# Two 64-key attentions of a pair as one walk over 64 tile slots, on one core

## The reference

```python
# second layer: softmax scale 1/sqrt(128); masks are given
sa  = attention(x, x, x, tgt_mask)                  # 16 heads of 8 features, 64 keys
out = layernorm(x + sa)
ca  = attention(ctx, ctx, out, src_mask)            # keys and values from ctx_1024
out = layernorm(out + ca)
# ... feed forward, gated fusion ...
# last layer: softmax scale 1/sqrt(8); no masks
q   = ln(x);  x = x + mha(q, q)
qc  = ln(x);  kv = ln(ctx);  x = x + mha(qc, kv)
# ... top-2 of 8 experts ...
```

## Time and profile before

| | |
|---|---|
| median of 3 runs | 2118.17 us (2116.89 to 2119.68) |
| the profiled execution's own time | 2117.3 us |
| its span in the trace | 2115.7 us |
| granted TensorE clock, mean over the span | 0.896 |
| PE busy in the span | 79% |
| DVE / ACT / POOL busy | 65% / 54% / 46% |

### The profile page before, as it was taken

One profiled execution on the slowest core, in us unless ns is written; L12 is line 12 of the kernel. 1 busy time (PEld: TensorE's weight loads), 2 busy tenths in 40 slices (PEclk: granted clock), 3 DMA queues, 4 the chain that ended last, 5 costly groups with the idle time before them and its releaser, 6 DMA issues. The chain is left out here.

```text
span 2115.7 us, 56320 instructions
## 1 busy us (share of the span) xinstructions
PE 1674.4 (79%) x17626; PEld 1301.0 (61%) x17626; DVE 1370.0 (65%) x4296; ACT 1142.8 (54%) x3291; POOL 963.3 (46%) x1443
## 2 busy tenths in 40 slices
PE   5899999999997799979897854599788972218882
PEld 5788888888866566656665712366566651217771
DVE  2677777777766488857776468677667852226773
ACT  1577777777753365546664322377567740007771
POOL 2344444444424355546665424344334434435773
PEclk9999999999998899989998967799879975559996
DMA  6776666666640222200000000000000000016665
GB/s 184 141 159 146 152 145 150 145 150 145 150 107 0 85 96 96 100 16 16 16 16 4 0 1 0 1 0 0 5 9 11 12 3 31 26 52 199 211 215 156
DMA packets 214507, 166.84 MB, mean 79 GB/s; under 512 B 27344, under 2 KB 188496, under 8 KB 214160
## 3 DMA queue, kind: packets, MB, share of 16 engines
q1 hardware_dynamic: 205840, 142.85, 27.0%
q0 software_dynamic: 8576, 22.88, 3.2%
HBM read 91.92 MB, written 73.76 MB: 78 GB/s over the span
## 5 line engine op out<-in xcount | busy, mean ns | idle before, releaser
L815 POOL TENSOR_TENSOR sb_work<-sb_work,sb_cols 128x512 f32<-128x512 f32 x128 | 134.4, 1050 | 316.2 <-ACT sb_work L1022 201.9
L678 ACT ACTIVATE sb_probs<-sb_probs,sb_work 128x128 f32<-128x128 f32 x512 | 198.7, 407 | 116.3 <-DVE sb_work L603 116.3
L953 DVE TENSOR_REDUCE sb_work<-PS 128x8 f32<-128x512 f32 x256 | 175.3, 685 | 87.2 <-PE PS L858 85.9
L257 POOL TENSOR_SCALAR sb_next_var_eps<-sb_next_moments 128x1 f32<-128x1 f32 (+1 forms) x184 | 43.9, 238 | 339.5 <-DVE sb_next_moments L252 338.8
L836 PE MATMUL PS<-sb_ident,sb_work 128*128 128x128 f32 x1024 | 168.4, 289 | 33.1 <-ACT sb_work L989 28.0
L989 ACT ACTIVATE sb_work<-sb_work 128x512 f32<-128x512 f32 x256 | 161.3, 630 | 60.3 <-DVE sb_work L955 59.2
L955 DVE TENSOR_TENSOR sb_work<-PS,sb_work 128x512 f32<-128x512 f32 x256 | 176.9, 691 | 8.8
L836 PEld LDWEIGHTS PS<-sb_ident,sb_work 128*128 128x128 f32 x1024 | 116.4, 145 | 69.7 <-ACT sb_work L989 55.1
L879 PE MATMUL PS<-sb_v_ones,sb_work 128*64 128x18 f32 x4096 | 146.5, 215 | 3.8 <-ACT sb_work L995 3.7
L879 PEld LDWEIGHTS PS<-sb_v_ones,sb_work 128*64 128x64 f32 x4096 | 134.0, 141 | 22.4 <-issue 10.2
L995 ACT ACTIVATE sb_work<-PS 128x512 f32<-128x512 f32 x256 | 139.8, 595 | 6.1 <-PE PS L836 2.5
(11 more groups left out here) (274 smaller groups left out, 4484.8 us busy)
## 6 DMA issues: line engine op xcount, KB each, us to landing
rel_scratch<-sb_work SPq DMA_DIRECT2D x64, 516.0 KB, 7.9
sb_work<-rel_scratch SPq DMA_DIRECT2D x64, 512.0 KB, 6.6
expert_rows<-sb_blank SPq DMA_DIRECT2D x36, 520.0 KB, 2.9
sb_w_up<-expert_halves SPq DMA_DIRECT2D x23, 512.0 KB
sb_w_down<-expert_halves SPq DMA_DIRECT2D x23, 512.0 KB
expert_halves<-sb_e_halves POOLq DMA_DIRECT2D x16, 512.0 KB, 5.9
sb_work<-expert_rows SPq DMA_DIRECT2D x23, 260.0 KB
sb_e_raw<-e_W POOLq DMA_DIRECT2D x16, 256.0 KB, 6.8
```

The source lines that it names most:

```text
L678: ins = e.activation(probs[:, j], probs[:, j], ACT.Exp, bias=neg_max[:, j:j + 1], scale=-1.0, accum_out=row_sum[:, j:j + 1])
L815: e.tensor_tensor(k_masked[:, u], k_sb[:, u].rearrange("p (b k) -> p b k", b=2).unsqueeze(2) .to_broadcast([P, 2, 4, S]), col("place").uns ...
L953: e.tensor_reduce(top, mine, AX.X, ALU.max).then_inc(sem("att_max_ready"), 1)
```

## The change

`PHASES` has eight entries instead of ten: `(AT, ATT[0:2])` and `(AT, ATT[2:4])` hold a pair each. `walk_pair` takes the place of `walk_late`: it counts n from -2 to 64, and each of the four roles gets the attention that its own tile slot belongs to (slots 0 to 31 the first, 32 to 63 the second). Steps 2 to 29 and 34 to 61 are hardware loops of two steps; steps -2 to 1, 30 to 33 and 62 to 64 are straight code. `meet` between the two attentions is gone. Instead DVE, in the head of every tile of the second attention, waits until POOL has kept the moments of the same tile of the first. SP still goes through the loads of the first attention and then through those of the second. Every semaphore and every buffer is the one of before.

```diff
+def walk_pair(e, pair, units, step):
+    def roles(n):
+        return [pair[t // units] if 0 <= t < 2 * units else None for t in (n + 2, n + 1, n, n - 1)]
+    def alone(n):
+        step(n // 2, n % 2, *roles(n))
+    for n in range(-2, 2):
+        alone(n)
+    with e.Fori(1, units // 2 - 1) as k:
+        for u in range(2):
+            step(k, u, *roles(2))
+    for n in range(units - 2, units + 2):
+        alone(n)
+    with e.Fori(units // 2 + 1, units - 1) as k:
+        for u in range(2):
+            step(k, u, *roles(units + 2))
+    for n in range(2 * units - 2, 2 * units + 1):
+        alone(n)
...
-        def att_sync(e, c):
+        def att_sync(e, pair):
+            for c in pair:
+                att_loads(e, c)
+
+        def att_loads(e, c):
...
-        def att_vector(e, c):
-            base = c["i"] * NT
-            cross, norm_cross = c["cross"], "cnorm" in c
-            if c["i"] == 0:
+        def att_vector(e, pair):
+            base = pair[0]["i"] * NT
+            if base == 0:
...
                 if head:
-                    m = n + 2
-                    at = bass.ds(m - base, 1)
+                    c, m = head, n + 2
+                    cross, t = c["cross"], m - c["i"] * NT
+                    at = bass.ds(t, 1)
                     mean = tile_mean[:, at]
                     wait(e, sem("att_transposed"), m - 1)
                     wait(e, sem("att_base_ready"), m - 1)
+                    if c is pair[1]:
+                        wait_alone(e, sem("x_moments_kept"), x_before[f"att{pair[0]['i']}"] + t + 1)
                     if "pre" in c:
-                        if norm_cross:
-                            e.wait_ge(sem(f"att_c_loaded{u}"), 16 * (cross * NT // 2 + k + 2))
+                        if "cnorm" in c:
+                            e.wait_ge(sem(f"att_c_loaded{u}"), 16 * ((cross - c["i"]) * NT // 2 + base // 2 + k + 2))
...
-            walk_late(e, NT, step)
+            walk_pair(e, pair, NT, step)
...
-        PHASES = [(L0, None), (FN, FFN[0]), (AT, ATT[0]), (AT, ATT[1]), (FN, FFN[1]), (L2, None), (AT, ATT[2]),
-                  (AT, ATT[3]), (ROUTE, None), (MOE, None)]
+        PHASES = [(L0, None), (FN, FFN[0]), (AT, ATT[0:2]), (FN, FFN[1]), (L2, None), (AT, ATT[2:4]),
+                  (ROUTE, None), (MOE, None)]
```

More of the change, by code:

```diff
@@ L789, in build, with att_pool, step @@
         values = PS[:, 5, 0:H * (HD + 1)].rearrange("p (h w) -> p h w", h=H)
-        def att_pool(e, c):
-            base = c["i"] * NT
-            cross = c["cross"]
-            def step(k, u, head, front, back, late=False):
+        def att_pool(e, pair):
+            base = pair[0]["i"] * NT
+            def step(k, u, head, front, back, late):
                 n = base + 2 * k + u
                 if head:
-                    m = n + 2
+                    c, m = head, n + 2
+                    t = m - c["i"] * NT
                     if c["mask"]:
-                        kk = (c["mi"] * NT) // 2 + k
+                        kk = (c["mi"] - c["i"]) * NT // 2 + base // 2 + k
                         e.wait_ge(sem(f"att_mask_loaded{u}"), 16 * (kk + 2))
@@ L861, in step @@
                 if head:
+                    c = head
+                    cross = c["cross"]
                     e.wait_ge(sem("att_normed"), n + 3)
@@ L890, in step @@
                     m = n + 2
+                    wq, wk, wv = (w_att[head["name"]][:, i] for i in range(3))
                     e.wait_ge(sem("att_T_kept"), m + 1)
@@ L903, in step @@
                     e.wait_ge(sem("att_ctxT_kept"), n)
[L904 removed]
+                    e.matmul(PS[:, 6, 3 * P:4 * P], att_ctxT[:, 1 - u], w_out[late["name"]][:, :], start=True, stop=True)\
                         .then_inc(sem("att_out_done"), 1)
[L906 to L911 removed]
+            walk_pair(e, pair, NT, step)
+        def att_vector(e, pair):
+            base = pair[0]["i"] * NT
+            if base == 0:
                 e.memset(v_ones[:, :], 0.0).then_inc(sem("att_v_zeroed"), 1)
```

59 lines of the change are left out of this document (30 added, 29 removed).

## The result

The changed kernel takes 2084.06 us (median of 5 runs, 2078.7 to 2087.5) against 2119.68 us of the kernel before beside it (5 runs, 2116.89 to 2122.74). The ratio is 0.9837 with the interval 0.9819 to 0.9855, so it is faster by 1.5 to 1.8%. The forecast was 2081.0 us. The profiled execution took 2078.7 us, of which 2077.1 are span.

What follows compares the result with a forecast made beforehand. TensorE was taken as the busiest engine, 79% of the span, with time lost at the seams. Savings of 15.2 + 23.3 - 1.3 = 37.2 us took 2117.3 to 2080.1, plus 0.87 for the median: 2081.0 us, range 2074 to 2091.

Steps and rivals of the forecast that it cites:

- The first seam: Where `msa` ends and `ca1` begins: four slots take 23.9 us instead of 39.15, saving 15.2 us.
- The ring of moments: In `ca1`, moments, load, transpose, projection, output product, moments again: sets 6.24 us per slot, unchanged by the new wait.
- The second seam: Where `sa` ends and `ca` begins: four slots at 5.60 us take 22.4 us instead of 45.70, saving 23.3.
- The clock at the seams: TensorE's clock where a pair's attentions join: taken as full, 1.00, because every step there has head work.
- rival A: Clock falls at the seams all the same: four second-seam slots at 8.12 us, 10.1 us lost, about 2091 us; chance 0.07.
- none above 1: Sign of being right: TensorE has no idle time above 1 us at the seams, where it had 2.90 and 4.93.
- The added wait: DVE's new wait in second attentions' heads: never holds, costs 0.09 us in 14 rounds of `ca`, 1.3 us in all.
- above 5.8: Sign of being wrong: a slot of `ca` above 5.8 us, where 5.60 to 5.65 us was expected.
- the price of one such addition: DVE, L938 to L941: 0.39 us straight, 0.48 us looped with a register instruction ahead of the wait, so 0.09 per step.
- rival C: Second loops, moved in DVE's list, fetch code every round: 1.7 us each, 48 us, so slower at 2129 us; chance 0.03.
- Rival B: DVE's new wait is dearer: 0.20 us per looped step, 56 steps, 11 us instead of 1.3, so 2091 us; chance 0.07.
- The total: Whole kernel: 37.2 us saved, profiled execution 2080.1 us, median 2081.0 us; chance 0.78 with its own range 2076 to 2086.

Runs made afterwards that it cites:

- the moved kernel: Changed kernel plus eight nops of DVE ahead of each pair's walk, outside all loops, against the changed kernel: 2083.55 us in one run.
- The kernel without overlap: Changed kernel with no meeting and the added wait kept, but each pair's attentions walked one after the other: 2113.82 us, ratio 1.0004 against before.

## Why the prediction was right, and where it was not

- **The first seam** was right: forecast 23.9 us as 2 x 5.68 + 2 x 6.27, measured 23.88 as 5.60 + 5.61 + 6.31 + 6.36. The ring of moments (27 waits of SP, 130.3 us, in the earlier trace rows) keeps its place: over the same 180 us of `ca1`, 933 to 1113 us in after, it is

```profile
SPq L77 <- DVE sb_c_moments L275: 131.5, 27, 5.2
```

  which is the same 27 waits, 1.2 us more in sum and none longer.
- **The second seam** was right to 0.8 us: forecast 22.4, measured 21.60. I had taken four slots at the 5.60 us of `ca`; the three slots 1503.90 to 1519.91 took 5.30 to 5.39 us, the pace of `sa`, which I had not looked up.
- **The clock at the seams** stayed at 1.00, so rival A fell where it had been placed, and no idle time of TensorE there is above 0.5 us (the prediction: none above 1). But the clock did fall in full steps of `ca`, a place that no step of mine had: in both profiles of this kernel it is at 0.50 from about 1533.5 to 1540, one slot takes 8.12 and 8.21 us and the next 5.92 and 5.87. In the moved kernel, with the same gaps in `ca`, these two slots are 6.38 and 5.50 us, so the fall cost 2.2 us. The idle time of TensorE ahead of it, 0.78 us, is no sufficient cause: the moved kernel has 0.78 us at the same step, and before with the wait 0.80, and both stay at 1.00. The kernel without overlap has 0.78 us without a fall, and a slot of 7.76 us four tiles later, behind an idle time of 0.50 us. What decides stays open.
- **The added wait** is the term that was mis-sized: "14 rounds x 0.09 = 1.3 us" for both attentions. Measured: `ca` +7.0 us (2.2 of it the fallen clock), and 9.2 us between the medians with and without it. A slot of `ca` is 5.85 us in the mean, and the prediction itself had named "above 5.8" as the sign of being wrong here. `ca1` is 0.5 and 1.4 us longer than before in the two profiles, but 1.2 us in the kernel without the wait too, so none of it can be put down to the wait. The step that failed is "the trace of before has the price of one such addition": those rows hold a register instruction and a wait, and for these 0.09 was fair (0.06 and 0.13 us measured). They hold no nop behind a wait, with which the gap at a round's head grows by 0.27 us more in `ca1` and 0.19 us in `ca`; and the 0.48 us were read in the middle of a step, not at a round's head, where no work covers it. The sum also had nothing for what an edit does to loops by moving them, which was left to rival C. In `ca1` the gap grew even more (+0.35 us at each head), and it cost nothing that can be seen: the stage takes 175.2 to 176.7 us in five profiles with the nop (176.9 without overlap), and 175.9 and 176.1 in the two joined ones without the wait. The ring that sets the pace there, as the prediction had it, is the likely reason.
- **Rival B** had 0.07 and was the true one in kind, 7 instead of 11 us. **Rival C** had the right object, the loops' place in DVE's list, with a wrong price and mechanism: 0.2 us per round in some loops and none in others, and no packets. The Trainium skill ("Runtime: NRT & Kernel Launch", section "Instruction fetch mechanics") lets the place of a branch's target matter, through a fetch of its code and without a price for it; the gaps of `sa` (0.47 or 0.72 us with the same body) agree that the place can matter, but the instruction queues moved no packet in rounds with the long gap, so a fetch by such packets is not what is seen.
- The Trainium skill ("VectorE: DVE Perf Modes", section "The DRAIN you can't avoid") says that a semaphore costs DVE nothing extra, from eight copies in a row with one behind each. It does not carry over to a wait on a register's value at a round's head: there the gap is 0.51 us without the wait, 0.57 with it, 0.76 with its nop.
- **The total** came out this near by luck, since errors cancel. The seams gave 0.9 us more than forecast, `ca1` and `ca` took 7.1 us more, and the profiled execution was 7.6 us better outside of the change, so it was 1.4 us below its forecast. Against the median, 2084.06 is 3.1 us above 2081.0; by the stages alone it would be 2118.2 - 31.0 = 2087.2 us.

## What to carry to other kernels

Where a pipeline is drained and refilled between two stages whose tiles depend one by one, price the seam from unit to unit in the trace: here four slots took 39 and 46 us instead of 24 and 22, and the meeting itself was 0.7 and 3.3 us of it. Before a wait goes into a loop, look whether a later wait on the same count already orders it, and price it at the loop's head, where its engine has no slack, with all that comes with it (here a nop). After an edit compare also the loops that it didn't touch: here some had 0.2 us more per round.

## What the runs showed of the hardware that I had not expected

- The same loop body on DVE has 0.47 to 0.50 or 0.72 us ahead of its first operation (`sa`), and 0.57 or 0.80 us (`ca`, wait without nop), depending on what stands ahead of it in the program. A shift by two instructions did it. These loops also have about 0.3 us more at their first turn (1.08 us where later rounds have 0.81).
- With a nop of its own behind a wait on a register's value, the gap at a round's head is longer than with the wait alone: 0.76 instead of 0.57 us in `ca`, 0.87 instead of 0.60 us in `ca1`. How much of that is place is not shown.
- Four, six or eight nops in a row in DVE's program are one instruction in what it runs.
- TensorE's granted clock fell from 1.00 to 0.50 in the middle of full steps, in which TensorE had been busy for 5.49 of 6 us (1524 to 1530), and stayed there for about 6.5 us, twice in two profiles of this kernel at the same slot, at a cost of 2.2 us each time. The same idle time of 0.78 us at the same step left it at 1.00 in the moved kernel.
- The second seam with its refill is no constant: 45.70 us before, and 39.6 and 39.8 us in two kernels that refill there in the same way, with the clock back at 1.00 two slots earlier.
